# Seven edge products per tile in place of eight: one 128-column operand for the first group, and an add on VectorE

## The chip, the cores and the metric

The kernel runs on one core of a Trainium2 chip. The metric is the device time of one launch in microseconds (us), as the median of several runs; lower is better.

## The reference, cut to what matters

There are 50,000 nodes with 256 features and 25,000 edges with 64 features, sorted by the node that they point to.

```python
h        = relu(layernorm(x))                        # (50000, 256)
agg      = segment_sum(edge_features, dst) / max(count, 1)   # (50000, 64)
combined = concat([agg, h], axis=1)                  # (50000, 320)
hidden   = relu(combined @ W1 + b1)                  # 320 -> 512
out      = x + hidden @ W2 + b2                      # 512 -> 256
```

## The kernel before

**Tiles.** The nodes are cut into 98 tiles of 512 (four groups of 128; the last tile has 336 nodes, three groups). Every engine runs its own program over the tiles, and semaphores tie them together. Every buffer of a tile's inputs exists twice.

**Precision.** Each fp32 factor is split into a high part, rounded to the fp32r type, and a low part, the rest. Products are taken as high x high, low x high and high x low, summed in PSUM.

**One tile on TensorE** (`step`, L861) is layer 1 in four blocks m = 0 to 3 of 128 hidden features: six products of 512 columns over the node features (`layer1_nodes`, L829 to L831), then two over the edge means (`layer1_means`, L838 and L839, which take the operands QA and QB). Between m = 1 and m = 2 stand the edge products of the next tile (`edge_means`, L818 and L819). Then come sixteen pairs for layer 2 (`layer2`, L852 with 512 columns and L854 with 256).

**The edge sums.** For each group of 128 nodes a window of 128 edges is loaded (ER) with a table (DT) of the target and of one over the count. GpSimd multiplies them (ES, L431), ScalarE rounds that to the high part (E_hi, L548), and GpSimd subtracts to get the low part (E_lo, L436). VectorE makes a one-hot matrix OH (L783) out of the targets. TensorE then forms, group by group, E_hi x OH and E_lo x OH into rows 0 to 63 of the PSUM bank PA, in the columns of that group: eight products of 128 columns with a 64-column stationary operand.

**From PA to layer 1.** ScalarE copies the rounded sum into QB rows 0 to 63 (`means_high`, L559) and from there into QA rows 0 to 63 (L561). VectorE writes the remainder, PA minus QB, into QA rows 64 to 127 (`means_low`, L678). `layer1_means` of m = 0 waits for both before L838 (L835, L836).

**VectorE's order** within a tile t is written by hand (`step`, L698): for m = 0 to 3 the low half of the hidden features (`hidden_low`, L682), with the statistics of tile t + 2 and the transposes of tile t + 1 (L666, L674) between them; then OH of tile t + 2; then the output of group 0 (`residual`, L693 and L696), `means_low` of tile t + 1, and the outputs of groups 1, 2 and 3. TensorE's m = 2 and m = 3 of the next tile wait for the outputs of groups 2 and 3, whose PSUM banks they write (L826).

**Who else waits for the outputs.** GpSimd adds the bias to the input of tile t + 2 (XB, L442) once all outputs of tile t are done. The DMA queue that SyncE issues, in order, stores tile t, waits for that XB, loads x of tile t + 4 and the edge windows of that tile (four pairs, L302 and L303), then waits for ScalarE's normalised features (HN, L542) and issues the four moves into HQ (L273) that the transposes read.

Of the kernel before, what the change touches and what calls it, by code (L numbers as in the profile page):

```python
# [5 lines left out]
ALU = mybir.AluOpType  # L6
ACT = mybir.ActivationFunctionType
AX_X = mybir.AxisListType.X
F32 = mybir.dt.float32
F32R = mybir.dt.float32r  # L10
# [4 lines left out]
P = 128  # L15
SUB = 4
# [4 lines left out]
def past(eng, sem, value):  # L21

    if not isinstance(value, int) or value > 0:
        eng.wait_ge(sem, value)


def build(nc, x, src, dst, edge_attr, w1, b1, w2, b2, out):
    N, D = x.shape
    E, DE = edge_attr.shape
# [38 lines left out]
    with ExitStack() as ctx:  # L68
        def sb(name, shape, dt=F32):
            return ctx.enter_context(nc.sbuf_tensor(name, shape, dt))  # L70

        def ps(name, shape, dt=F32):
            return ctx.enter_context(nc.psum_tensor(name, shape, dt))

        def sem(name):
            return ctx.enter_context(nc.semaphore(name))
# [57 lines left out]
        rel = [sb(f"rel{b}", [P, SUB]) for b in range(2)]  # L134

        ES = [sb(f"ES{b}", [P, SUB, DE]) for b in range(2)]
        E_hi = [sb(f"E_hi{b}", [P, SUB, DE], F32R) for b in range(2)]
        E_lo = [sb(f"E_lo{b}", [P, SUB, DE], F32R) for b in range(2)]
        OH = [sb(f"OH{b}", [P, SUB, P], F32R) for b in range(2)]
        HT = sb("HT", [P, CD, TILE])  # L140
        HT_hi = sb("HT_hi", [P, CD, TILE], F32R)
# [1 line left out]
        QA = sb("QA", [P, TILE], F32R)  # L143
        QB = sb("QB", [P, TILE], F32R)
# [26 lines left out]
        PA = ps("PA", [P, TILE])  # L171
# [16 lines left out]
        def groups(t):  # L188

            return range(GROUPS if isinstance(t, int) and t == TILES - 1 else SUB)  # L190
# [38 lines left out]
        s_ehi = sem("s_ehi")  # L229
        s_es = sem("s_es")  # L230
        s_elo = sem("s_elo")
# [4 lines left out]
        s_hhi = sem("s_hhi")  # L236
        s_hlo = sem("s_hlo")
        s_qhi = sem("s_qhi")
        s_qlo = sem("s_qlo")
        s_l1 = sem("s_l1")  # L240
        s_1hi = sem("s_1hi")
# [144 lines left out]
        def _(pool):  # L386
# [46 lines left out]

            def edges_low(t, b):
                pool.wait_ge(s_ehi, t + 1)
                pool.tensor_tensor(E_lo[b][:], ES[b][:], E_hi[b][:], ALU.subtract).then_inc(s_elo, 1)  # L436

            def residual_in(t, b):

# [14 lines left out]
            with pool.If(flag != 0):  # L454
# [35 lines left out]
                with pool.Fori(0, BLOCKS) as i:  # L490
# [5 lines left out]
                    pool.wait_ge(s_gout, 16 * i + 16)  # L496
            edges_scaled(0, 0)
            edges_low(0, 0)
            pool.wait_ge(s_b2, 16)
            residual_in(0, 0)  # L500
            edges_scaled(1, 1)
            edges_low(1, 1)
            residual_in(1, 1)
            for t in range(2):
                norm(t + 2, t % 2)
                edges_scaled(t + 2, t % 2)
                edges_low(t + 2, t % 2)
                residual_in(t + 2, t % 2)
# [9 lines left out]
        def _(act):  # L518
# [26 lines left out]
            def edges_high(t, b):  # L545
                act.wait_ge(s_es, t + 1)
                past(act, s_sum, t - 1)
                act.activation(E_hi[b][:], ES[b][:], ACT.Copy).then_inc(s_ehi, 1)  # L548

            def transposed_high(t):  # L550
                past(act, s_l1, CH * t)
# [29 lines left out]
            layernorm(0, 0)  # L581
            transposed_high(0)
            edges_high(0, 0)
            means_high(0)
            layernorm(1, 1)
            edges_high(1, 1)
            for t in range(2):
                hidden_high(t)
                transposed_high(t + 1)
                means_high(t + 1)  # L590
                layernorm(t + 2, t % 2)
                edges_high(t + 2, t % 2)
# [14 lines left out]
        def _(dve):  # L607
# [67 lines left out]

            def means_low(t):
                dve.wait_ge(s_qhi, 2 * t + 1)
                dve.tensor_tensor(QA[DE:P, :], PA[0:DE, :], QB[0:DE, :], ALU.subtract).then_inc(s_qlo, 1)  # L678

            def hidden_low(t, m):  # L680
                dve.wait_ge(s_1hi, CH * t + m + 1)
# [16 lines left out]
            def step(t, b, later=True, latest=True):  # L698
                hidden_low(t, 0)
                if latest:  # L700
                    stat(t + 2, b, (0, 1))
                hidden_low(t, 1)
                if latest:
                    stat(t + 2, b, (2, 3))
                hidden_low(t, 2)
                if latest:
                    aggregate(t + 2, b)
                    if isinstance(t, int):
                        ends(t + 2, b)
                if later:  # L710
                    transpose(t + 1, 1 - b, 0)
                hidden_low(t, 3)
                if later:
                    transpose(t + 1, 1 - b, 1)
                    transposed_low(t + 1)
                if latest:
                    onehot(t + 2, b)
                residual(t, b, 0)
                if later:
                    means_low(t + 1)  # L720
                for j in groups(t)[1:]:
                    residual(t, b, j)
# [64 lines left out]
            ends(0, 0)  # L787
            onehot(0, 0)
            means_low(0)
            ends(1, 1)  # L790
            onehot(1, 1)
# [10 lines left out]
        def _(pe):  # L802
# [8 lines left out]
            def edge_means(t, b):  # L811
                pe.wait_ge(s_oh, SUB * t + SUB)
                pe.wait_ge(s_elo, t + 1)
                past(pe, s_qhi, 2 * t)
                past(pe, s_qlo, t)
                for k in groups(t):
                    cols = slice(k * P, (k + 1) * P)
                    pe.matmul(PA[0:DE, cols], E_hi[b][:, k, :], OH[b][:, k, :], start=(k == 0), stop=False)  # L818
                    last = pe.matmul(PA[0:DE, cols], E_lo[b][:, k, :], OH[b][:, k, :], start=False, stop=(k == groups(t)[-1]))  # L819
                last.then_inc(s_sum, 1)  # L820

            def layer1_nodes(t, m):
# [18 lines left out]
            def layer2(t):  # L841

                for j, ms in ((0, (0, 1, 2)), (1, (0, 1, 2)), (0, (3,)), (1, (3,)), (2, (0, 1, 2, 3)), (3, (0, 1, 2, 3))):
                    if j not in groups(t):
                        continue
                    rows = slice(j * P, min((j + 1) * P, nodes(t).stop))
                    some = slice(0, rows.stop - rows.start)
                    for m in ms:
                        if j == 0:
                            pe.wait_ge(s_1lo, CH * t + m + 1)  # L850

                        pe.matmul(out_bank(j)[some, :], H1_hi[:, m, rows], w2_both[:, m, :, :].rearrange("p a d -> p (a d)"),  # L852
                                  start=(m == 0), stop=False)
                        last = pe.matmul(out_bank(j)[some, 0:D], H1_lo[:, m, rows], w2_both[:, m, 0, :],  # L854
                                         start=False, stop=(m == CH - 1))
                    if m == CH - 1:
                        last.then_inc(s_l2, 1)
                    if j == 2 and isinstance(t, int) and t == 0:
                        edge_means(1, 1)

            def step(t, b, later=True):  # L861
                for m in range(CH):
                    if not (isinstance(t, int) and t == 0):
                        layer1_nodes(t, m)
                    layer1_means(t, m)
                    if m == 1 and later and not (isinstance(t, int) and t == 0):
                        edge_means(t + 1, 1 - b)
                layer2(t)
# [4 lines left out]
            for j in range(SUB):  # L873
                pe.wait_ge(s_ln, j + 1)
                for c in range(CD):
                    last = pe.transpose(P2[c][:, j * P:(j + 1) * P], HN[0][:, j, c * P:(c + 1) * P], ident[:])
# [13 lines left out]
            layer1_nodes(0, 2)  # L890
            layer1_nodes(0, 3)
            edge_means(0, 0)
            pe.wait_ge(s_wlo, 2)
            pe.wait_ge(s_ones, 1)
# [31 lines left out]
```

## Time and profile before

| | us |
|---|---|
| median of 3 runs (lowest, highest) | 1372.71 (1372.31, 1373.8) |
| the profiled execution, its own time | 1373.5 |
| its span, first to last instruction | 1371.9 |
| TensorE matmul busy | 1334.5 (97%) |
| VectorE busy | 1193.2 (87%) |
| ScalarE busy | 695.3 (51%) |
| GpSimd busy | 536.9 (39%) |
| mean granted TensorE clock | 0.987 of full |

Matmuls are pipelined: the duration of one (390 ns at 512 columns) includes the time through the array, and the next one starts before it ends. What a matmul costs is the distance from its start to the start of the next one. PEld is the row of weight loads, which run beside the matmul ahead of them. Times in a timeline are counted from the span's start.

### The profile page before, as it was taken

How to read it: one execution, taken by the hardware profiler on the slowest of the kernel's cores; microseconds unless marked ns; L12 is line 12 of the kernel's file. 1: busy time of each engine (PE TensorE's matmuls, PEld its weight loads, DVE VectorE, ACT ScalarE, POOL GpSimd, SP SyncE). 2: the span in 40 equal slices, each digit the busy share in tenths (PEclk: the TensorE clock that was granted, in tenths of full speed). 3: DMA queues.
4: the chain of work that ended last, by engine and by line, in shares of the span. 5: the costliest groups of instructions: out<-in, count | busy, mean ns of one | idle time of the engine just before them, and what ended most of it. 6: DMA issues, size and time to landing. Idle time of an engine off the chain costs nothing.

```text
span 1371.9 us, 29802 instructions
## 1 busy us (share of the span) xinstructions
PE 1334.5 (97%) x7066; PEld 1121.0 (82%) x7066; DVE 1193.2 (87%) x2963; ACT 695.3 (51%) x1281; POOL 536.9 (39%) x708
## 2 busy tenths in 40 slices
PE   2799999999999999999999999999999999999999
PEld 1588888888888888888888888888888888888887
DVE  6498989898989888898989898988889898989897
ACT  2354545454555555454545455555545454545553
POOL 4334343434344343434343434334343434343431
PEclk6899999999999999999999999999999999999999
DMA  4355454545455554545454545555454545454542
GB/s 92 77 131 136 113 145 108 143 111 139 116 134 122 128 131 119 132 117 144 107 145 110 140 114 135 119 131 129 121 132 118 139 110 146 108 142 113 136 108 75
DMA packets 422628, 168.59 MB, mean 123 GB/s; under 512 B 321092, under 2 KB 422230, under 8 KB 422616
## 3 DMA queue, kind: packets, MB, share of 16 engines
q1 hardware_dynamic: 420916, 166.49, 49.6%
q10 hardware_dynamic: 1700, 1.97, 0.6%
q14 instruction: 9, 0.07, 0.0%
q8 instruction: 3, 0.05, 0.0%
HBM read 66.12 MB, written 51.40 MB: 86 GB/s over the span
## 4 chain that ended last, share of the span: by engine, by line
PE 96%; DVE 1%; DMA 1%; SPq 1%; issue 0%; ACT 0%; POOL 0%; DVEq 0%; POOLq 0%
PE P L852 27%; PE P L829 14%; PE P L854 14%; PE P L831 13%; PE P L830 13%; PE P L838 6%; PE P L839 6%; PE PA L818 2%; PE PA L819 2%; DMA dst_w<-in_dst_dram 1%; DVE wb_lo L737 0%; SPq L273 0%; DVE wb_lo L736 0%; ACT HN L542 0%; SPq L301 0%
## 5 line engine op out<-in xcount | busy, mean ns | idle before, releaser
L852 PE MATMUL P<-w_both,H_hi 128*128 128x512 f32 x1564 | 559.9, 399 | 8.4 <-DVE H_lo L682 8.4
L568 ACT ACTIVATE H_hi<-P 128x512 fp32r<-128x512 f32 x392 | 233.2, 596 | 510.1 <-PE P L839 510.1
L854 PE MATMUL P<-w_both,H_lo 128*128 128x256 f32 x1564 | 441.0, 282 | 0.0
L682 DVE SCALAR_TENSOR_TENSOR H_lo<-P,H_hi 128x512 fp32r<-128x512 f32 x392 | 268.4, 685 | 113.5 <-ACT H_hi L568 103.6
L852 PEld LDWEIGHTS P<-w_both,H_hi 128*128 128x128 f32 x1564 | 295.1, 189 | 82.0 <-DVE H_lo L682 10.0
L829 PE MATMUL P<-HT_hi,w_hi 128*128 128x512 f32 (+1 forms) x784 | 314.2, 401 | 4.2 <-DVE HT_lo L674 4.2
L831 PE MATMUL P<-HT_hi,w_lo 128*128 128x512 f32 (+1 forms) x784 | 308.7, 394 | 0.0
L830 PE MATMUL P<-HT_lo,w_hi 128*128 128x512 f32 (+1 forms) x784 | 305.8, 390 | 0.0
L854 PEld LDWEIGHTS P<-w_both,H_lo 128*128 128x128 f32 x1564 | 294.9, 189 | 3.7
L442 POOL TENSOR_TENSOR XB<-X,b_row 128x1024 f32<-128x1024 f32 x98 | 236.6, 2414 | 136.0 <-DVE O L696 136.0
L436 POOL TENSOR_TENSOR E_lo<-ES,E_hi 128x256 fp32r<-128x256 f32 x98 | 73.2, 747 | 412.2 <-ACT E_hi L548 412.2
L666 DVE STREAM_TRANSPOSE HT<-HQ 128x512 f32<-128x512 f32 x194 | 209.5, 1080 | 0.0
L542 ACT ACTIVATE HN<-X,shift,rstd 128x256 f32<-128x256 f32 x392 | 202.3, 587 | 3.8 <-POOL shift L425 3.8
L554 ACT ACTIVATE HT_hi<-HT 128x512 fp32r<-128x512 f32 x194 | 122.8, 633 | 123.1 <-DVE HT L666 123.1
L696 DVE TENSOR_TENSOR O<-P,XB 128x256 f32<-128x256 f32 x391 | 166.0, 425 | 13.3
L831 PEld LDWEIGHTS P<-HT_hi,w_lo 128*128 128x128 f32 x784 | 147.7, 188 | 34.0
L829 PEld LDWEIGHTS P<-HT_hi,w_hi 128*128 128x128 f32 x784 | 148.0, 189 | 31.8 <-issue 4.6
L830 PEld LDWEIGHTS P<-HT_lo,w_hi 128*128 128x128 f32 x784 | 148.5, 189 | 25.2
L693 DVE TENSOR_TENSOR XB<-P,XB 128x256 f32<-128x256 f32 x391 | 163.4, 418 | 4.6 <-PE P L854 1.5
L838 PE MATMUL P<-QA,wa_hi 128*128 128x512 f32 x392 | 153.1, 390 | 1.6 <-DVE QA L678 1.6
L839 PE MATMUL P<-QB,wb_lo 128*128 128x512 f32 x392 | 152.7, 389 | 0.0
L674 DVE TENSOR_TENSOR HT_lo<-HT,HT_hi 128x512 fp32r<-128x512 f32 x194 | 135.0, 696 | 15.4 <-ACT HT_hi L554 9.2
(74 smaller groups left out, 1136.5 us busy)
## 6 DMA issues: line engine op xcount, KB each, us to landing
HQ<-HN SPq DMA_DIRECT2D x388, 128.0 KB, 3.1
out_dram<-O SPq DMA_DIRECT2D x97, 512.0 KB, 3.3
X<-in_x_dram SPq DMA_DIRECT2D x96, 512.0 KB, 3.4
ER<-in_edge_attr_dram SPq DMA_DIRECT2D x392, 32.0 KB, 1.7
DT<-table_dram SPq DMA_DIRECT2D x392, 1.0 KB, 1.7
X<-in_x_dram ACTq DMA_DIRECT2D x1, 512.0 KB, 6.1
w_raw<-in_L_gnn_W_dram ACTq DMA_DIRECT2D x4, 128.0 KB, 6.1
w_raw<-in_L_gnn_W_dram ACTq DMA_DIRECT2D x2, 256.0 KB, 8.2
```

The source lines that it names most:

```text
L442: pool.tensor_tensor(XB[b][:], X[b][:], b2_row[:].unsqueeze(1).to_broadcast([P, SUB, D]), ALU.add).then_inc(s_xb, 1)
L542: act.activation(into, rows, ACT.Relu, bias=shift[b][:, j:j + 1], scale=rstd[b][:, j:j + 1]).then_inc(s_ln, 1)
L568: act.activation(H1_hi[:, m, nodes(t)], bank(m)[:, nodes(t)], ACT.Relu).then_inc(s_1hi, 1)
L666: dve.transpose(HT[:, c, :].rearrange("p (j n k) -> p k j n", j=SUB, k=QN), HQ[b][:, :, c * QP:(c + 1) * QP].rearrange("p (k j) f -> p k j ...
L682: dve.scalar_tensor_tensor(out=H1_lo[:, m, nodes(t)], in0=bank(m)[:, nodes(t)], scalar=0.0, in1=H1_hi[:, m, nodes(t)], op0=ALU.max, op1=AL ...
L829: pe.matmul(bank(m)[:, nodes(t)], w1_hi[:, c, cols], HT_hi[:, c, nodes(t)], start=(c == 0), stop=False)
L830: pe.matmul(bank(m)[:, nodes(t)], w1_hi[:, c, cols], HT_lo[:, c, nodes(t)], start=False, stop=False)
L831: pe.matmul(bank(m)[:, nodes(t)], w1_lo[:, c, cols], HT_hi[:, c, nodes(t)], start=False, stop=False)
L838: pe.matmul(bank(m)[:, nodes(t)], wa_hi[:, cols], QA[:, nodes(t)], start=False, stop=False)
L839: pe.matmul(bank(m)[:, nodes(t)], wb_lo[:, cols], QB[:, nodes(t)], start=False, stop=True).then_inc(s_l1, 1)
L852: pe.matmul(out_bank(j)[some, :], H1_hi[:, m, rows], w2_both[:, m, :, :].rearrange("p a d -> p (a d)"), start=(m == 0), stop=False)
L854: last = pe.matmul(out_bank(j)[some, 0:D], H1_lo[:, m, rows], w2_both[:, m, 0, :], start=False, stop=(m == CH - 1))
```

## The change

The high and low parts of a tile's edges are laid side by side in one buffer, E_both. For the first group of a tile, both lie in one stationary operand of 128 columns, and one product writes the high sums into rows 0 to 63 of PA and the low sums into rows 64 to 127, columns 0 to 127. Groups 1 to 3 are multiplied as before. VectorE first takes the remainder for all 512 columns as before, waits for its own result, and then adds rows 64 to 127 of PA to the first 128 columns of it.

```diff
-        E_hi = [sb(f"E_hi{b}", [P, SUB, DE], F32R) for b in range(2)]
-        E_lo = [sb(f"E_lo{b}", [P, SUB, DE], F32R) for b in range(2)]
+        E_both = [sb(f"E_both{b}", [P, SUB, 2, DE], F32R) for b in range(2)]
...
             def edges_low(t, b):
                 pool.wait_ge(s_ehi, t + 1)
-                pool.tensor_tensor(E_lo[b][:], ES[b][:], E_hi[b][:], ALU.subtract).then_inc(s_elo, 1)
+                pool.tensor_tensor(E_both[b][:, :, 1, :], ES[b][:], E_both[b][:, :, 0, :], ALU.subtract).then_inc(s_elo, 1)
...
-                act.activation(E_hi[b][:], ES[b][:], ACT.Copy).then_inc(s_ehi, 1)
+                act.activation(E_both[b][:, :, 0, :], ES[b][:], ACT.Copy).then_inc(s_ehi, 1)
...
             def means_low(t):
                 dve.wait_ge(s_qhi, 2 * t + 1)
-                dve.tensor_tensor(QA[DE:P, :], PA[0:DE, :], QB[0:DE, :], ALU.subtract).then_inc(s_qlo, 1)
+                dve.tensor_tensor(QA[DE:P, :], PA[0:DE, :], QB[0:DE, :], ALU.subtract).then_inc(s_qpart, 1)
+                dve.wait_ge(s_qpart, t + 1)
+                dve.tensor_tensor(QA[DE:P, 0:P], PA[DE:P, 0:P], QA[DE:P, 0:P], ALU.add).then_inc(s_qlo, 1)
...
-                for k in groups(t):
+                pe.matmul(PA[:, 0:P], E_both[b][:, 0, :, :].rearrange("p a d -> p (a d)"), OH[b][:, 0, :],
+                          start=True, stop=True)
+                for k in groups(t)[1:]:
                     cols = slice(k * P, (k + 1) * P)
-                    pe.matmul(PA[0:DE, cols], E_hi[b][:, k, :], OH[b][:, k, :], start=(k == 0), stop=False)
-                    last = pe.matmul(PA[0:DE, cols], E_lo[b][:, k, :], OH[b][:, k, :], start=False, stop=(k == groups(t)[-1]))
+                    pe.matmul(PA[0:DE, cols], E_both[b][:, k, 0, :], OH[b][:, k, :], start=(k == 1), stop=False)
+                    last = pe.matmul(PA[0:DE, cols], E_both[b][:, k, 1, :], OH[b][:, k, :], start=False,
+                                     stop=(k == groups(t)[-1]))
                 last.then_inc(s_sum, 1)
```

## Rows read from the trace of the kernel before

**Rows 1.** The page: busy time, and TensorE's busy tenths in 40 slices.

```profile
PE 1334.5 (97%) x7066; PEld 1121.0 (82%) x7066; DVE 1193.2 (87%) x2963; ACT 695.3 (51%) x1281; POOL 536.9 (39%) x708
...
PE   2799999999999999999999999999999999999999
```

**Rows 2.** Busy time in two tile steps: us, engine busy (instructions), clock, DMA share.

```profile
700.41:713.93 13.52, 13.52 (x73) 11.40 (x72) 12.16 (x31) 7.05 (x13) 5.36 (x7) 1.00 0.51 127
713.93:727.45 13.52, 13.52 (x73) 11.39 (x72) 11.91 (x31) 7.05 (x13) 5.36 (x7) 1.00 0.52 126
```

**Rows 3.** Timeline of TensorE's matmuls: start us, us, engine, line, what.

```profile
714.17 0.39 PE L839 MATMUL P<-QB,wb_lo 128*128 128x512 f32 x1
714.39 0.22 PE L818 MATMUL PA<-OH,E_hi 128*64 128x128 f32 x1
...
714.87 0.45 PE L829 MATMUL P<-HT_hi,w_hi 128*128 128x512 f32 x1
715.16 0.39 PE L830 MATMUL P<-HT_lo,w_hi 128*128 128x512 f32 x1
```

**Rows 4.** Timeline of the weight loads in the same stretch.

```profile
714.17 0.13 PEld L818 LDWEIGHTS PA<-OH,E_hi 128*64 128x64 f32 x1
714.39 0.14 PEld L819 LDWEIGHTS PA<-OH,E_lo 128*64 128x64 f32 x1
...
714.81 0.19 PEld L829 LDWEIGHTS P<-HT_hi,w_hi 128*128 128x128 f32 x1
714.92 0.19 PEld L830 LDWEIGHTS P<-HT_lo,w_hi 128*128 128x128 f32 x1
```

**Rows 5.** Timeline of VectorE, with the idle time before an instruction in brackets.

```profile
710.64 0.68 DVE L678 TENSOR_TENSOR QA<-PA,QB 64x512 fp32r<-64x512 f32 x1
711.36 0.42 DVE L693 TENSOR_TENSOR XB<-P,XB 128x256 f32<-128x256 f32 x1
...
713.74 0.68 DVE L682 SCALAR_TENSOR_TENSOR H_lo<-P,H_hi 128x512 fp32r<-128x512 f32 x1
...
717.60 0.69 DVE L682 SCALAR_TENSOR_TENSOR H_lo<-P,H_hi 128x512 fp32r<-128x512 f32 x1 [1.02 <-ACT H_hi L568]
```

**Rows 6.** Groups by form: what other sizes and strides take (busy us, mean ns).

```profile
L852 PE MATMUL P<-w_both,H_hi 128*128 128x512 f32 x1560 | 558.5, 399 | 8.4 <-DVE H_lo L682 8.4
...
L852 PE MATMUL P<-w_both,H_hi 128*80 128x512 f32 x4 | 1.4, 390 | 0.0
...
L619 DVE TENSOR_TENSOR rel<-DT,base 128x4 f32<-128x4 f32 x98 | 15.0, 153 | 8.3 <-DMA DT<-table_dram 7.0 <-issue 1.3
L696 DVE TENSOR_TENSOR O<-P,XB 128x256 f32<-128x256 f32 x390 | 165.6, 425 | 13.3
L450 POOL TENSOR_TENSOR w_both<-w_raw,w_both 128x1024 fp32r<-128x1024 f32 x1 | 2.8, 2794 | 0.0
L448 POOL TENSOR_TENSOR w_lo<-w_raw,w_hi 128x1024 fp32r<-128x1024 f32 x1 | 2.4, 2356 | 0.0
```

**Rows 7.** Timelines of the first weight load that reads QA, and of GpSimd's E_lo.

```profile
711.88 0.19 PEld L838 LDWEIGHTS P<-QA,wa_hi 128*128 128x128 f32 x1
...
711.81 0.75 POOL L436 TENSOR_TENSOR E_lo<-ES,E_hi 128x256 fp32r<-128x256 f32 x1 [4.15 <-ACT E_hi L548]
```

**Rows 8.** Timelines at the start: VectorE's H_lo, and the load released by it.

```profile
43.35 0.69 DVE L682 SCALAR_TENSOR_TENSOR H_lo<-P,H_hi 128x512 fp32r<-128x512 f32 x1 [1.63 <-ACT H_hi L568]
...
44.10 0.19 PEld L852 LDWEIGHTS P<-w_both,H_hi 128*128 128x128 f32 x1 [1.55 <-DVE H_lo L682]
```

**Rows 9.** Waits of SyncE's DMA queue, 100 to 1300 us: total us, times, longest.

```profile
SPq L24 <- POOL XB L442: 103.4, 89, 1.4
SPq L273 <- ACT HN L542: 59.3, 89, 0.7
```

**Rows 10.** The chain in order of time, at the start: start us, us, what.

```profile
39.31 0.60 ACT QB L559
...
55.57 0.79 PE P L852
```

More of the change, by code:

```diff
@@ L238, in build @@
         s_qhi = sem("s_qhi")
+        s_qpart = sem("s_qpart")
         s_qlo = sem("s_qlo")
```

## The prediction

> **What bounds the kernel now.** I read the page first, then the busy time of single tile steps, then the timelines of each engine around the edge products. The page says that TensorE is busy 97% of the span, at nine tenths or more in all but the first two slices, and the clock granted in a step is full [rows 1, 2]. The reader is to see in the table of two tile steps that a step lasts 13.52 us and that matmuls fill all of it; VectorE comes next with 12.16 and 11.91 us, ScalarE has 7.05 and GpSimd 5.36 [rows 2]. So in the steady state every microsecond comes from the distance between one matmul and the next, and nothing else counts unless it makes TensorE wait. VectorE's idle time is little, though: most of it is one wait of 1.02 us a tile, for ScalarE's H_hi of block m = 2 [rows 5]. An edit that gives TensorE less and VectorE more has to be judged by both.
>
> **TensorE: one product less.** The eight edge products start at 714.39 and the next line at 714.87, so one takes 0.48 / 8 = 0.06 us [rows 3]. The change removes one from each tile, the last one included (six become five): 98 x 0.06 = 5.9 us.
>
> Does the wide product cost more than a narrow one? Its pass is still 128 columns of OH, and a pass hardly depends on the stationary columns: L852 takes 390 ns with 80 of them and 399 ns with 128 [rows 6]. Its weight load is longer. Seven loads of 64 columns take the 0.42 us from 714.39 to 714.81, 0.06 us each, against 0.11 us (714.81 to 714.92) after a load of 128 [rows 4]. A load of 0.11 us shows if the pass ahead of it lasts only 0.06 us, and this is what happens at the end of the block: L829 starts at 714.87 by its record, but it lasts 0.45 instead of 0.39 us, and L830 follows after 0.29 us, some 0.06 late [rows 3]. The wide product isn't in that place. It stands first, behind L839, whose pass has 512 columns: the load of the first edge operand starts at 714.17, and its product at 714.39 [rows 3, 4]. That is 0.22 us for a load of 0.11 us. So the wide load costs nothing; without that cover it would cost 0.05 us, which would eat the gain. The late start of L829 behind the block stays as it is. I take 0.06 us a tile as saved; the bounds are 0.01 (wide load in the open) and 0.06.
>
> The Trainium skill has the same thing as a rule (TensorE: Matmul & The Clock Gate, section "LDWEIGHTS (loading the stationary operand)"): a weight load takes its number of columns divided by 1.2 ns, so the width of the operand matters and not its rows. By that, 128 columns take 107 ns and 64 take 53 ns; the trace agrees with its 0.11 and at most 0.06 us. By the rule alone, putting high and low in one operand would save no load time at all, since one load of 107 ns replaces two of 53; the sum would be zero if the edge block were bound by loads throughout. It is the long pass ahead of the first load that decides.
>
> **VectorE: one add more.** No row has 64 x 128. The two-input operations take 153 ns at 4 columns and 425 ns at 256 [rows 6]; a straight line between them gives 0.28 us at 128. L678 ends at 711.32 and the next one starts at 711.36, so a hand-over costs 0.03 to 0.04 us [rows 5]. The add is also behind a wait for L678, so it can't overlap it: 0.32 us a tile. Bounds: 0.20 us if it overlapped its follower, and 0.72 us (all of L678's distance to the next) if rows 64 to 127 of PSUM or the fp32r output made it as slow as L678.
>
> Where the 0.32 us go:
> - *The path to L838.* QA is complete at 711.32, and the load of L838 starts at 711.88 [rows 5, 7], when TensorE's own order comes to it (no idle time is noted in front of it). A release by VectorE costs about 0.06 us (H_lo ends at 44.04, the load that it frees starts at 44.10) [rows 8]. The slack is thus 0.56 - 0.06 = 0.50 us, and 0.18 us are left. No stall.
> - *What is queued behind it on VectorE:* the outputs of groups 1 to 3 and H_lo of m = 0 and 1 come 0.32 us later. H_lo of m = 2 then waits about 0.3 us less of its 1.02 us [rows 5], and from there VectorE is again where it was against TensorE. So the delay doesn't add up over tiles. All outputs are done when H_lo of m = 0 starts, at 713.74 now and at 714.06 then, and L829 of m = 2, the first product that writes a bank freed by them, starts at 714.87 [rows 3, 5].
> - *GpSimd and the DMA queue.* XB of the next tile but one starts 0.32 us later, so the queue's wait for it (103.4 us in 89 waits, 1.2 us each) grows, and the windows behind it are issued later. The queue then has 0.7 us of waiting for HN in each tile (59.3 us in 89), which shrinks to about 0.35 us [rows 9]. The moves into HQ go out at the same time as before. The slack of this ring is 0.7 us, more than that of L838.
> - E_both has a stride of two. For GpSimd a strided second input and output cost 2794 against 2356 ns at 1024 elements in four runs [rows 6], so L436 with four runs may take 0 to 0.44 us more. E_lo ends at 712.56 now, and the load of its first use starts at 714.17 [rows 4, 7]: covered by 1.6 us, and by nothing else of GpSimd, which is idle 8 us a tile [rows 2].
>
> So VectorE's part, the stride and the new semaphore cost nothing on the path.
>
> The Trainium skill adds a reason why the add can't hide in its neighbours (VectorE: DVE Perf Modes, section "Two Vector instructions with no wait between them"): an instruction whose input or output starts in another quadrant of partitions than the last one is held until all earlier ones are done. The trace agrees for L678, which writes from partition 64: its follower starts 0.72 us behind it, after its full 0.68 us. By the rule the price is 0.32 us, and without it down to 0.20 us; both are under the slack.
>
> **The start and the end.** The chain at the start runs from the edge sums of tile 0 over ScalarE's QB (39.31) and the windows of the queue to L852 at 55.57 [rows 10]. QB starts 0.06 us earlier, as the block is shorter, so this tile's saving passes down the chain; the added 0.32 us lie beside ScalarE's work there. At the end VectorE's last H_lo are released by TensorE through ScalarE. Nothing to add.
>
> **Sum.** 98 x 0.06 = 5.9 us. The profiled execution has 1373.5 us and a span of 1371.9, so it would show 1367.6 and 1366.0. It lies 0.8 us above the median of the runs, 1372.71; the predicted median is 1372.7 - 5.9 = 1366.8 us, 0.43% faster. A change of 0.2% (2.7 us) is about what a measurement of this kernel can tell from none.
>
> **Rivals.**
> 1. *The wide load shows.* If the first edge load can't run under L839's pass, the product costs 0.11 instead of 0.06 us: saved 0.01 us a tile, 1 us in all, 1371.7 us. For it: L829 behind the block shows just this. Against it: the first load starts 0.22 us ahead of its product [rows 4]. Chance 0.08, with whatever else halves the gain, such as a stall of 0.03 us a tile at L838.
> 2. *The add lands on TensorE's path.* It decides from 0.50 us a tile on. At the upper bound of 0.72 us, TensorE waits 0.72 - 0.50 = 0.22 us at L838 in each tile and saves 0.06: 0.16 x 97 = 15 us more, 1388 us, slower. For it: VectorE is at 89% in a step, and L838 has the smallest slack of all. Against it: a quarter of the columns of L678, and the two-input operations of rows 6 lie on a line. Chance 0.05.
> 3. *The change doesn't shorten the block,* because something beside the products sets its length, such as a wait ahead of it. Then nothing is saved, 1372.7 us. Against it: the load of the first edge operand starts right with the pass of L839, and the eight products follow at even distances up to L829. Chance 0.02.
>
> **Numbers.** Forecast 0.85; its own range is 1365.8 to 1368.2 (the rounding of 0.06 by 0.005 is 0.5 us, and the runs lie 1.5 us apart). Rival 1 has 0.08, rival 2 0.05, rival 3 0.02. To leave out no more than 2 in 10 the range goes from 1365.6 to 1369.2 us, which takes in half a gain. Faster by over 0.2%: 0.85, the forecast. Within 0.2%: 0.11, rivals 1 and 3 and a stall at L838 just over the 0.50 us. Slower: 0.04, the rest of rival 2.
>
> **What would show each step.** In the changed kernel a tile step lasts 13.46 us, still full of matmuls. The first edge product starts behind L839 at 0.22 us, the second 0.06 us later, and the next L829 0.42 us after the first. The add has about 285 ns. The load of L838 stands where it stood, with no idle time of TensorE ahead of it and QA complete 0.2 us ahead. VectorE's wait for H_hi at m = 2 is 0.6 to 0.8 us. The prediction is wrong if TensorE has idle time ahead of L838, if the second edge product comes over 0.1 us behind the first, or if a step still lasts 13.5 us.

## The result and the profile after

The changed kernel takes 1364.82 us (median of 4 runs, 1363.79 to 1365.96) against 1372.51 us before: a ratio of 0.9944, 95% interval 0.9927 to 0.9961. That is 7.7 us less where 5.9 were forecast, and 0.8 us below the lower end of the range. Measured once more beside other kernels, it took 1365.31 us against 1372.42, 7.1 us less, ratio 0.9948 (0.9935 to 0.9962).

The page of the changed kernel, to read against [rows 1]: the span, and busy time. TensorE has 98 matmuls and 6.2 us less, VectorE 98 instructions and 20.2 us more.

```profile
span 1363.6 us, 29704 instructions
...
PE 1328.3 (97%) x6968; PEld 1120.1 (82%) x6968; DVE 1213.4 (89%) x3061; ACT 695.3 (51%) x1281; POOL 537.5 (39%) x708
```

The same two tile steps as in [rows 2], each still full of matmuls, with VectorE at 12.38 and 12.10 us where it had 12.16 and 11.91:

```profile
696.31:709.76 13.45, 13.45 (x75) 11.39 (x73) 12.38 (x32) 7.05 (x14) 5.37 (x8) 1.00 0.53 127
709.76:723.20 13.44, 13.44 (x75) 11.38 (x73) 12.10 (x32) 7.05 (x13) 5.35 (x8) 1.00 0.52 127
```

TensorE's timeline around the edge block, the lines of [rows 3]. L818 is the wide product, L834 the first product behind the block:

```profile
709.33 0.39 PE L844 MATMUL P<-QB,wb_lo 128*128 128x512 f32 x1
709.56 0.22 PE L818 MATMUL PA<-OH,E_both 128*128 128x128 f32 x1
709.62 0.22 PE L822 MATMUL PA<-OH,E_both 128*64 128x128 f32 x1
...
709.98 0.44 PE L834 MATMUL P<-HT_hi,w_hi 128*128 128x512 f32 x1
710.26 0.39 PE L835 MATMUL P<-HT_lo,w_hi 128*128 128x512 f32 x1
```

The wide product starts 0.23 us behind L844 and the narrow one 0.06 us behind it; the block takes 0.42 us instead of 0.48. Its weight load stands under L844's pass, and the load of L834 is still the one that shows (the lines of [rows 4]):

```profile
709.33 0.19 PEld L818 LDWEIGHTS PA<-OH,E_both 128*128 128x128 f32 x1
709.56 0.13 PEld L822 LDWEIGHTS PA<-OH,E_both 128*64 128x64 f32 x1
...
709.92 0.19 PEld L834 LDWEIGHTS P<-HT_hi,w_hi 128*128 128x128 f32 x1
710.03 0.19 PEld L835 LDWEIGHTS P<-HT_lo,w_hi 128*128 128x128 f32 x1
```

VectorE's timeline (the lines of [rows 5]), and the first weight load that waits for QA (the line of [rows 7]):

```profile
705.80 0.68 DVE L678 TENSOR_TENSOR QA<-PA,QB 64x512 fp32r<-64x512 f32 x1
706.52 0.30 DVE L680 TENSOR_TENSOR QA<-PA,QA 64x128 fp32r<-64x128 f32 x1
706.85 0.42 DVE L695 TENSOR_TENSOR XB<-P,XB 128x256 f32<-128x256 f32 x1
...
712.69 0.69 DVE L684 SCALAR_TENSOR_TENSOR H_lo<-P,H_hi 128x512 fp32r<-128x512 f32 x1 [0.87 <-ACT H_hi L568]
```

```profile
707.04 0.19 PEld L843 LDWEIGHTS P<-QA,wa_hi 128*128 128x128 f32 x1
```

The add puts 0.33 us between L678 and its old follower. QA is complete at 706.82, 0.22 us ahead of the load. VectorE's wait at m = 2 shrinks from 1.02 to 0.87 us.

The waits of the DMA queue from 100 to 1300 us, the lines of [rows 9]: it waits longer for XB and less for HN, 0.30 us a tile instead of 0.67.

```profile
SPq L24 <- POOL XB L442: 133.3, 89, 1.7
SPq L273 <- ACT HN L542: 26.5, 89, 0.3
```

**Where the 8.3 us of the two profiled spans lie.** The first edge product of tile 2 and that of the last tile mark the steady part. These are the two lines of the kernel before:

```profile
65.43 0.22 PE L818 MATMUL PA<-OH,E_hi 128*64 128x128 f32 x1
...
1349.83 0.22 PE L818 MATMUL PA<-OH,E_hi 128*64 128x128 f32 x1
```

and of the changed kernel:

```profile
64.12 0.22 PE L818 MATMUL PA<-OH,E_both 128*128 128x128 f32 x1
...
1341.55 0.22 PE L818 MATMUL PA<-OH,E_both 128*128 128x128 f32 x1
```

Between them lie 95 tile steps: 1284.40 us against 1277.43, so 13.520 against 13.447 us a step, 0.073 us less and 7.0 us in all. The part behind them takes 22.08 and 22.01 us by the unrounded times: the last tile's one product less. The 1.3 us ahead of them is the start. Of these, 0.8 us are there already at the first edge product of tile 0 (38.63 us before, 37.82 us after), ahead of every product that the change takes away. The stretch of 59 to 61 us shows one reason for the rest (us, busy of PE, PEld, DVE, ACT, POOL, clock, DMA share, GB/s); first before, then after:

```profile
59.00:61.00 2.00, 2.00 (x15) 1.82 (x15) 0.45 (x2) 0.43 (x1) 0.00 (x0) 0.71 0.13 17
```

```profile
59.00:61.00 2.00, 2.00 (x14) 1.75 (x13) 1.05 (x3) 1.71 (x4) 0.00 (x0) 1.00 0.11 17
```

TensorE's clock went from 1.2 to 2.4 GHz within this stretch before, and ahead of it after. The start spreads from run to run: the three kernels of experiments 9 to 11, alike but for a few columns of one product, reach the mark at 64.63, 65.57 and 65.55 us. So the question left by the result is the step: 0.073 us where the prediction had 0.060.

### The profile page after: what moved, and what is told of

The parts are those of the page before. It is cut to its first block, busy times and chain, and to the rows that moved or that the text cites. A ratio compares the mean times of both kernels' runs of the same rounds, so it can differ in the third digit from the quotient of the medians.

```text
span 1363.6 us, 29704 instructions
## 1 busy us (share of the span) xinstructions
PE 1328.3 (97%) x6968; PEld 1120.1 (82%) x6968; DVE 1213.4 (89%) x3061; ACT 695.3 (51%) x1281; POOL 537.5 (39%) x708
## 4 chain that ended last, share of the span: by engine, by line
PE 96%; DVE 1%; DMA 1%; SPq 1%; issue 0%; ACT 0%; POOL 0%; DVEq 0%; POOLq 0%
PE P L857 27%; PE P L859 14%; PE P L834 14%; PE P L836 13%; PE P L835 13%; PE P L843 6%; PE P L844 6%; PE PA L823 1%; PE PA L822 1%; DMA dst_w<-in_dst_dram 1%; PE PA L818 0%; DVE wb_lo L739 0%; SPq L273 0%; DVE wb_lo L738 0%; ACT HN L542 0%
## 5 line engine op out<-in xcount | busy, mean ns | idle before, releaser
L834 PE MATMUL P<-HT_hi,w_hi 128*128 128x512 f32 (+1 forms) x784 | 312.6, 399 | 4.2 <-DVE HT_lo L674 4.2
L436 POOL TENSOR_TENSOR E_both<-ES,E_both 128x256 fp32r<-128x256 f32 x98 | 73.0, 745 | 411.1 <-ACT E_both L548 411.1
L698 DVE TENSOR_TENSOR O<-P,XB 128x256 f32<-128x256 f32 x391 | 166.1, 425 | 13.3
L834 PEld LDWEIGHTS P<-HT_hi,w_hi 128*128 128x128 f32 x784 | 147.8, 189 | 32.2 <-issue 4.6
L695 DVE TENSOR_TENSOR XB<-P,XB 128x256 f32<-128x256 f32 x391 | 163.5, 418 | 4.6 <-PE P L859 1.5
L844 PE MATMUL P<-QB,wb_lo 128*128 128x512 f32 x392 | 153.3, 391 | 0.0
```

Source lines behind the costliest of these rows:

```text
L834: pe.matmul(bank(m)[:, nodes(t)], w1_hi[:, c, cols], HT_hi[:, c, nodes(t)], start=(c == 0), stop=False)
L844: pe.matmul(bank(m)[:, nodes(t)], wb_lo[:, cols], QB[:, nodes(t)], start=False, stop=True).then_inc(s_l1, 1)
```

## The experiments

Three theories of the 0.013 us. A: a product costs 0.060 us and the rest is spread. B: the length of the block shifts a pattern in the distances between starts, whatever products it holds. C: the wide operand or the new buffer saves it. Each step length below is the distance between the same two marks over 95.

**1. Seven narrow products, nothing else changed.**

```diff
-                    pe.matmul(PA[0:DE, cols], E_hi[b][:, k, :], OH[b][:, k, :], start=(k == 0), stop=False)
-                    last = pe.matmul(PA[0:DE, cols], E_lo[b][:, k, :], OH[b][:, k, :], start=False, stop=(k == groups(t)[-1]))
+                    last = pe.matmul(PA[0:DE, cols], E_hi[b][:, k, :], OH[b][:, k, :], start=(k == 0),
+                                     stop=(k == groups(t)[-1]))
+                    if k < len(groups(t)) - 1:
+                        last = pe.matmul(PA[0:DE, cols], E_lo[b][:, k, :], OH[b][:, k, :], start=False, stop=False)
```

> The kernel before with the last edge product (low edges of a tile's last group) left out, so those low edges are missing from the sums; no wide operand, no new buffer, no add. Theory A (a product costs its 0.060 us, the rest of the gain is the start's spread): a steady tile step of 13.460 us, 5.9 us less in all. Theory B (the block of seven ends on another phase of a pattern in TensorE's start distances, and the next matmuls come 0.013 us closer): 13.447 us a step, as in the changed kernel, and about 7 us less in all. Theory C (the wide operand or the new buffer's layout saves the extra 0.013 us): 13.460 us here.

Measured: 1365.67 us against 1372.76, ratio 0.995 (0.9934 to 0.9967). The marks in TensorE's timeline:

```profile
65.48 0.22 PE L818 MATMUL PA<-OH,E_hi 128*64 128x128 f32 x1
...
1342.91 0.22 PE L818 MATMUL PA<-OH,E_hi 128*64 128x128 f32 x1
```

The step is 1277.43 / 95 = 13.447 us, that of the changed kernel. C falls: the whole gain in the step comes from having seven products, and the wide operand is only the way to get there with the sums complete. Of A the second half falls, as the extra 0.013 us is in the step and not in the start. B stands, but this step length alone would also fit a product that simply costs 0.073 us.

The traces show where in the step the 0.013 us lie. These two products stand four distances behind the end of the block, which is at 714.87 us before and at 709.98 us after; first before, then the changed kernel:

```profile
715.85 0.39 PE L830 MATMUL P<-HT_lo,w_hi 128*128 128x512 f32 x1
```

```profile
710.94 0.39 PE L835 MATMUL P<-HT_lo,w_hi 128*128 128x512 f32 x1
```

As means over 85 steps, with the trace's times taken to the nanosecond: the block goes from 0.478 to 0.418 us (0.419 in this experiment), so the product itself is worth 0.060 us. The four distances behind it go from 0.982 to 0.968 us (0.968 here), though their products have the same columns as before. The rest of the step stays at 12.060 us, within 0.001.

**2. Without the add.** `means_low` has only its first instruction, as before the change.

> The changed kernel without the second add on VectorE, so the first group's low sums are missing from the result. If the add is wholly covered: 13.447 us a step, the same time as the changed kernel within 1 us. VectorE's wait for H_hi of m = 2 goes back to about 1.0 us. If the add costs something on the path, this kernel is faster by that.

Measured: 1365.35 us against 1372.76, ratio 0.995 (0.9933 to 0.9966), with a step of 13.447 us (marks at 64.36 and 1341.79). VectorE's wait at m = 2 is 0.95 us in a tile. The changed kernel took 1365.31 with the add. The add is covered.

**3. The wide product last.**

```diff
-                pe.matmul(PA[:, 0:P], E_both[b][:, 0, :, :].rearrange("p a d -> p (a d)"), OH[b][:, 0, :],
-                          start=True, stop=True)
                 for k in groups(t)[1:]:
...
+                last = pe.matmul(PA[:, 0:P], E_both[b][:, 0, :, :].rearrange("p a d -> p (a d)"), OH[b][:, 0, :],
+                                 start=True, stop=True)
                 last.then_inc(s_sum, 1)
```

> The changed kernel with the wide product last in the block, behind a pass of 128 columns in place of L839's 512. By the cover argument the wide load now shows: its product comes 0.11 us behind the one ahead instead of 0.06, 0.05 us a step more (13.50 us), 5 us more in all. If the load's width didn't matter, 13.447 us.

Measured: 1371.0 us against 1372.76, ratio 0.9993 (0.9983 to 1.0002). TensorE's timeline at the end of the block:

```profile
711.99 0.22 PE L821 MATMUL PA<-OH,E_both 128*64 128x128 f32 x1
712.05 0.28 PE L823 MATMUL PA<-OH,E_both 128*128 128x128 f32 x1
712.16 0.44 PE L834 MATMUL P<-HT_hi,w_hi 128*128 128x512 f32 x1
```

The wide product takes 0.28 us by its record, and the line behind it starts 0.11 us later, not 0.06. By the marks (63.38 and 1346.51 us) the step is 13.507 us, 0.060 more than with the wide product first. In the block itself the wide load now costs 0.053 us (0.472 against 0.418 us, means over 85 steps), as expected; the other 0.007 us lie in the distances behind it. So 0.060 of the gain of 0.073 us hangs on the pass of 512 columns ahead of the wide load.

**4. The add twice.**

```diff
-                dve.wait_ge(s_qpart, t + 1)
+                dve.wait_ge(s_qpart, 2 * t + 1)
+                dve.tensor_tensor(QA[DE:P, 0:P], PA[DE:P, 0:P], QA[DE:P, 0:P], ALU.add).then_inc(s_qpart, 1)
+                dve.wait_ge(s_qpart, 2 * t + 2)
                 dve.tensor_tensor(QA[DE:P, 0:P], PA[DE:P, 0:P], QA[DE:P, 0:P], ALU.add).then_inc(s_qlo, 1)
```

> The changed kernel with the add done twice in a row, each behind a wait for the one before, so the first group's low sums count double. VectorE has 0.33 us more per tile. By the slack of 0.50 us with 0.33 used by the first add, two adds (0.66 us) overrun it by 0.16 us: TensorE idles about 0.16 us ahead of the first product that reads QA in every tile, a step of 13.61 us, 15 us more in all. If QA isn't what TensorE waits for first, 13.447 us still.

Measured: 1371.25 us against 1372.76, ratio 0.9987 (0.9978 to 0.9997), with a mean step of 13.502 us (marks at 65.52 and 1348.20). VectorE's second add, the load that waits for it, and the matmuls around it:

```profile
710.94 0.30 DVE L682 TENSOR_TENSOR QA<-PA,QA 64x128 fp32r<-64x128 f32 x1
```

```profile
711.29 0.19 PEld L845 LDWEIGHTS P<-QA,wa_hi 128*128 128x128 f32 x1 [0.20 <-DVE QA L682]
711.40 0.19 PEld L846 LDWEIGHTS P<-QB,wb_lo 128*128 128x128 f32 x1
```

```profile
711.13 0.40 PE L838 MATMUL P<-HT_hi,w_lo 128*128 128x512 f32 x1
711.36 0.43 PE L845 MATMUL P<-QA,wa_hi 128*128 128x512 f32 x1
```

The load is 0.16 us later than the start of L838, where it would stand without the wait. That is the overrun expected (0.66 less 0.50). But a step loses only 0.055 us, not 0.16, and the whole kernel 5.9 us against the changed one, not 15. The load takes 0.11 us of a pass of 0.23, so by estimate it may come 0.12 us late before the product does. That puts TensorE's slack for QA at 0.62 us, not 0.50; the added 0.66 us less the 0.055 lost give 0.61.

**5, 6 and 12. Six, nine and five narrow products,** by leaving out more low products or doing the last one twice.

> The kernel before with the low products of a tile's last two groups left out (six edge products, low edges of those groups missing from the sums). Theory A (a product is worth its 0.060 us): two less save 0.120, a step of 13.400 us. Theory B (what a product is worth alternates with the phase on which the block ends; 0.0733 for the eighth): the second one is worth less than 0.060, about 0.047, and the step is about 13.400, or 0.0733 again with 13.373 if the price of a product is simply 0.073.

> The kernel before with the last low product done twice (nine edge products, those low edges counted double). Theory A: 13.520 + 0.060 = 13.580 us a step. Theory B: another value that isn't 0.073 above 13.520, since the eight of the kernel before already stand on the late phase. If each product is simply worth 0.073, 13.593 us.

> The kernel before with the low products of a tile's last three groups left out (five edge products). The steps for six to nine products are 13.400, 13.447, 13.520, 13.573 us, 0.058 us a product in the mean with swings of 0.015. With the same mean and swings: 13.342 plus or minus 0.015 us; with the first theory's fixed 0.060, 13.340.

The marks, for six, nine and five products:

```profile
64.80 0.22 PE L818 MATMUL PA<-OH,E_hi 128*64 128x128 f32 x1
...
1337.80 0.22 PE L818 MATMUL PA<-OH,E_hi 128*64 128x128 f32 x1
```

```profile
63.36 0.22 PE L818 MATMUL PA<-OH,E_hi 128*64 128x128 f32 x1
...
1352.82 0.22 PE L818 MATMUL PA<-OH,E_hi 128*64 128x128 f32 x1
```

```profile
63.19 0.22 PE L818 MATMUL PA<-OH,E_hi 128*64 128x128 f32 x1
...
1329.85 0.22 PE L818 MATMUL PA<-OH,E_hi 128*64 128x128 f32 x1
```

The last three columns split the step, in us, as means over 85 steps:

| edge products | step, us | worth of the last one, us | block | four distances behind it | rest |
|---|---|---|---|---|---|
| 5 | 13.333 | | 0.301 | 0.975 | 12.057 |
| 6 | 13.400 | 0.067 | 0.359 | 0.982 | 12.059 |
| 7 | 13.447 | 0.047 | 0.419 | 0.968 | 12.060 |
| 8 (before) | 13.520 | 0.073 | 0.478 | 0.982 | 12.060 |
| 9 | 13.573 | 0.053 | 0.541 | 0.975 | 12.057 |

The mean over four is 0.060 us, the prediction's figure. What a step gains by a single one swings between 0.047 and 0.073, and the change removed the dearest. The product itself doesn't swing so: within the block one is worth 0.058 to 0.062 us. Most of the swing lies in the distances behind the block. In whole times, single runs or few: 1361.28 us with six (2 runs), 1378.36 with nine (5 runs, ratio 1.0045, 1.0032 to 1.0058) and 1353.32 with five (1 run).

**7. The changed kernel again,** unchanged, beside 5, 6 and 8.

> The changed kernel as it is, again, for the same chip as its neighbours: 13.447 us a step. By 95 steps of 0.073 us and the start and end (three tiles of 0.06 us) it is 7.1 us faster than before, 1365.6 us against 1372.7; if the first result's 7.7 us was more than the spread of the start, 7.7 again.

1365.31 us against 1372.42 (5 and 12 runs): 7.1 us, the sum of 95 steps of 0.073 us and three products at the two ends. The 0.6 us more of the first result is within the spread of runs of one kernel, 1371.29 to 1373.82 us here.

**8. Four wide products,** one for each group, with an add of all 512 columns and `means_low` ahead of the output of group 0.

```diff
-                residual(t, b, 0)
                 if later:
                     means_low(t + 1)
+                residual(t, b, 0)
...
+                    last = pe.matmul(PA[:, cols], E_both[b][:, k, :, :].rearrange("p a d -> p (a d)"), OH[b][:, k, :],
+                                     start=True, stop=True)
```

> All four groups in a wide product each (four products instead of seven), one add of all 512 columns, and on VectorE the means ahead of group 0's output instead of behind it, which gives them 0.9 us more room. Wide loads behind passes of 128 columns show: 3 x 0.1125 + 0.06 = 0.40 us to the record of the next line against 0.42 for seven. So 0.02 us less a step: 13.42 to 13.43 us, 1 to 2 us in all faster than the changed kernel. Rival: VectorE now has 0.40 us more per tile (its wait for H_hi falls from 0.85 to about 0.4 us), the moves of the DMA queue come 0.1 us later as its slack of 0.3 us is used up, and a step isn't shorter or even longer.

Measured: 1363.24 us (1362.82 to 1365.1) against 1372.42, ratio 0.9935 (0.9922 to 0.9949). The marks:

```profile
63.05 0.22 PE L822 MATMUL PA<-OH,E_both 128*128 128x128 f32 x1
...
1339.22 0.22 PE L822 MATMUL PA<-OH,E_both 128*128 128x128 f32 x1
```

and TensorE's timeline of the four products, in one line, and the product behind them:

```profile
707.85 0.56 PE L822 MATMUL PA<-OH,E_both 128*128 128x128 f32 x4
708.24 0.45 PE L837 MATMUL P<-HT_hi,w_hi 128*128 128x512 f32 x1
```

The four take 0.39 us, against 0.42 for seven. The step is 13.433 us (13.42 to 13.43 expected), 0.013 less than in the changed kernel, 1.3 us over the steady part. The medians are 2.1 us apart, but the runs of the two kernels overlap (the changed one has 1364.73 to 1366.03), so the step is the firmer figure. The rival falls: the queue's wait for HN is gone and VectorE's wait at m = 2 is down to 0.46 us in a tile, yet TensorE doesn't wait in the steady part. It is the fastest complete kernel here, by little.

**9 to 11. L839 of m = 3 cut to 504, 496 and 480 columns** in the kernel before (`some` is the columns without the last 8, 16 or 32).

```diff
-                pe.matmul(bank(m)[:, nodes(t)], wb_lo[:, cols], QB[:, nodes(t)], start=False, stop=True).then_inc(s_l1, 1)
+                some = slice(0, min(nodes(t).stop, TILE - 8)) if m == 3 else nodes(t)
+                pe.matmul(bank(m)[:, some], wb_lo[:, cols], QB[:, some], start=False, stop=True).then_inc(s_l1, 1)
```

> The kernel before with the means product L839 of m = 3 cut from 512 to 504 columns, so the last 8 nodes of a tile miss that term. 8 of 512 columns at the full clock are 3.3 us a thousand (0.0033 us). If the distances between starts are smooth, a step lasts 13.5167 us. If a step's length moves only in stages (all seven steps so far are multiples of 0.00667 us), 13.5200 or 13.5133, or a jump as large as the extra 0.013 us of the seventh product.

> The same product cut to 496 columns (last 16 nodes miss the term). Smooth: 13.5133 us a step. In stages: a value off this by up to 0.013 us.

> The same product cut to 480 columns (last 32 nodes miss the term). Smooth: 13.5067 us a step. In stages: a value off this by up to 0.013 us.

The marks for 504, 496 and 480 columns:

```profile
64.63 0.22 PE L818 MATMUL PA<-OH,E_hi 128*64 128x128 f32 x1
...
1347.13 0.22 PE L818 MATMUL PA<-OH,E_hi 128*64 128x128 f32 x1
```

```profile
65.57 0.22 PE L818 MATMUL PA<-OH,E_hi 128*64 128x128 f32 x1
...
1349.33 0.22 PE L818 MATMUL PA<-OH,E_hi 128*64 128x128 f32 x1
```

```profile
65.55 0.22 PE L818 MATMUL PA<-OH,E_hi 128*64 128x128 f32 x1
...
1348.68 0.22 PE L818 MATMUL PA<-OH,E_hi 128*64 128x128 f32 x1
```

The steps are 13.500, 13.513 and 13.507 us, where a smooth rule would give 13.517, 13.513 and 13.507. Eight columns less save 0.020 us, sixteen 0.007, thirty-two 0.013. Sixteen and thirty-two follow the smooth rule; eight don't, and so the shortest cut saves most. The traces show where: the part with layer 1 behind the block shrinks as the columns do (0.003, 0.007 and 0.013 us), but with 504 columns the first three distances of layer 2, right behind the cut product, are 0.568 us together, where they are 0.584 in the other two and before. This is B's pattern with no edge product touched. One run each, but the step is a mean over 95.

## Why the prediction was right and where it was wrong

- **What bounds the kernel:** right. The steps before and after are full of matmuls, and every change of the whole time is found again in the distance between starts.
- **TensorE, one product less, "one takes 0.48 / 8 = 0.06 us ... 98 x 0.06 = 5.9 us":** this is the term that failed, by its size. The mechanism held, and so did the 0.06 us within the block (0.478 to 0.418). What failed is "The late start of L829 behind the block stays as it is": the sum put the distances behind the block at nothing, without a reason, and they fell by 0.014 us (experiment 1). So a step saves 0.073 us, and 95 steps give 7.0 us and not 5.7. With two other counts of products the same term would have been off the other way (0.047 and 0.053 us in experiments 5 and 6). The range allowed 0.005 for rounding, and the bounds of the saving, 0.01 and 0.06, took in none above 0.06. Of the 1.8 us by which the first result beats the forecast, 1.3 are this; the other 0.5 are the start's spread.
- **The wide load costs nothing first in the block and 0.05 us without cover:** right, 0 us (experiment 1, with no wide load, has the same step) and 0.053 us in the block, 0.060 in the step (experiment 3). The rival that the load shows would have left 0.013 us a step. The trace agrees with the rule of the Trainium skill on weight loads (TensorE: Matmul & The Clock Gate, "LDWEIGHTS (loading the stationary operand)"): with four wide products (experiment 8) loads of 128 columns set the spacing, three distances of 0.11 us in the 0.39 us of the block.
- **The add, 0.28 us and a hand-over:** right, 0.295 and 0.33 us in all (the straight line gives 0.287, which the prediction wrote as 0.28), the upper bound of 0.72 us far off. The add started only behind the whole of L678, for which it waits. Its follower L695 has no wait for the add, and still started only behind the whole of it (706.82 and 706.85 us); the next L695 started at 707.65 us, 0.34 us behind an L698 of 0.42. The rule of the Trainium skill on quadrants (VectorE: DVE Perf Modes, "Two Vector instructions with no wait between them") says the same of the follower, and the trace agrees. For the add itself no run here separates the rule from the wait.
- **Its path to L838, slack 0.50 us:** the release was read rightly (0.22 us are left), the slack was some 0.1 us too small. The load had been put down as the deadline, and it is the product (experiment 4). The rival of a stall would have decided from about 0.6 us on.
- **VectorE, GpSimd and the DMA queue absorb the delay:** right. The wait at m = 2 is 0.87 us where 0.6 to 0.8 were named, as part of the delay is taken up ahead of H_lo of m = 1 (1.26 us behind H_lo of m = 0, where it stood 1.48 behind). The queue keeps 0.30 us. The stride of E_both costs GpSimd nothing: 745 ns against the 747 of before.
- **The start and the end:** the end adds nothing beyond its one product. The start gave 1.3 us in the profiled pair. That this is spread and not the change rests on the 0.8 us that are there before the first product saved, and on experiment 7, where the medians differ by what the steps and three products give.
- **The third rival,** that the block doesn't get shorter: wrong, it went from 0.48 to 0.42 us.

The cause of the extra 0.013 us is thus shown as far as its place: the distances right behind the block. What stays open is what makes the pattern. All steps measured without a stall are whole multiples of 0.00667 us, to the nanosecond; the runs show this and don't explain it.

## What to carry to other kernels

Where matmuls are packed without a gap, the price of one is its average only over several: ask for the step with one, two and three of them more or less, before a saving of 0.06 us in 13.5 is counted to a tenth, and look at the distances behind the change as well as at those within it. In these runs a weight load of 128 columns behind a pass of 128 cost 0.05 us; behind one of 512 it was free, so the place of a wide operand decides whether merging two narrow ones gains anything. And slack for an operand ends at the product that uses it: the load's own slack under the pass ahead (0.12 us here) is to be added.

## What was unexpected of the hardware

- The distance between the starts of back-to-back matmuls isn't a function of their own columns. Of otherwise equal kernels, 504 columns gave a shorter step (13.500 us) than 496 (13.513) and 480 (13.507), and one edge product less brought the four unchanged products behind the block 0.014 us closer.
- The profiled runs, whose programs hardly differ up to there, reached the mark in tile 2 between 63.05 and 65.57 us. That is 2.5 us of the whole time that no change to the steady part explains; the first edge product of tile 0 already spreads from 36.91 to 38.78 us.
